# A four-block transformer on one core: TensorE's order in the tile loop around the gate of the first expert layer

## What is computed

```python
x = x + tanh(g_xattn[0]) * attention(layernorm(x), mask, ctx)       # 32 heads of 8, rotary, second softmax over ctx
x = x + tanh(g_ffn[0])   * top1_experts(layernorm(x))               # 8 experts, 256 -> 256, gate = softmax
x = x + tanh(g_xattn[1]) * wkv(layernorm(x), ctx)                   # recurrence over the 64 rows
x = x + tanh(g_ffn[1])   * top2_experts(layernorm(x))               # 8 experts, 256 -> 704 -> 256
```

## Time and profile before

| | |
|---|---|
| median of three runs | 498.18 us |
| profiled execution: its own time, its span | 498.84 us, 496.7 us |
| granted TensorE clock, mean | 0.994 |
| busy: TensorE (matmul), its weight loads, VectorE, ScalarE, GpSimd | 93%, 70%, 76%, 52%, 35% |
| tiles 1 to 6 on TensorE | about 52 to 249 us, 33.5 us each |

### The profile page before, as it was taken

How to read it: one execution, slowest core, us unless ns; L and a number is a source line. 1 busy time by engine, 2 the same in 40 slices (tenths; PEclk the granted TensorE clock), 3 DMA queues, 4 the chain that set the end, 5 groups by cost and what they waited for, 6 DMA issues and landing times. The chain is left out here.

```text
span 496.7 us, 10389 instructions
## 1 busy us (share of the span) xinstructions
PE 461.7 (93%) x3123; PEld 347.1 (70%) x3124; DVE 376.7 (76%) x1007; ACT 259.4 (52%) x562; POOL 175.8 (35%) x228
## 2 busy tenths in 40 slices
PE   4979999998999999999989999999999999999993
PEld 2648677686686776866857755566777878788782
DVE  5876788998988889989877889767867566566540
ACT  2765384572752845737513343326565766657641
POOL 4134213225124232241131160315446557555522
PEclk9999999999999999999999899999999999999998
DMA  7951304004022040040130689648566767768511
GB/s 217 287 107 29 63 1 86 18 13 86 22 44 53 21 84 15 12 84 16 38 69 21 255 341 366 193 116 298 170 205 215 251 183 245 223 197 252 162 22 21
DMA packets 24769, 63.37 MB, mean 128 GB/s; under 512 B 5176, under 2 KB 15296, under 8 KB 21792
## 3 DMA queue, kind: packets, MB, share of 16 engines
q1 hardware_dynamic: 19456, 56.38, 37.2%
q0 software_dynamic: 4416, 6.03, 6.6%
q10 hardware_dynamic: 864, 0.54, 0.3%
HBM read 48.79 MB, written 5.24 MB: 109 GB/s over the span
## 5 line engine op out<-in xcount | busy, mean ns | idle before, releaser
L2021 PE MATMUL bank_o<-w,hT 128*128 (+1 forms) x276 | 68.3, 389 | 1.9 <-issue 1.0
L1406 DVE TENSOR_TENSOR wl<-lw,wh 128x1024 fp32r<-128x1024 f32 (+1 forms) x54 | 60.9, 1129 | 1.1 <-ACT wh L639 1.1
L2021 PEld LDWEIGHTS bank_o<-w,hT 128*128 128x128 f32 (+1 forms) x276 | 48.8, 189 | 16.2 <-issue 11.4
L639 ACT ACTIVATE wh<-lw 128x1024 fp32r<-128x1024 f32 (+1 forms) x54 | 52.9, 981 | 1.8 <-DMA lw<-in_w 1.8
L1091 DVE TENSOR_REDUCE mx<-bank_s 128x8 f32<-128x512 f32 x64 | 42.6, 687 | 11.0 <-PE bank_s L1756 10.7
L498 POOL TENSOR_SCALAR rstd<-mv 128x1 f32<-128x1 f32 x32 | 9.3, 289 | 111.5 <-DVE mv L1011 111.5
L1754 PE MATMUL bank_s<-Kh,Qx 128*128 128x128 f32 x256 | 40.9, 282 | 1.5 <-DVE mx L1091 1.0
L593 POOL DMA_INDIRECT out_x<-ys,idx_out x18 | 29.0, 1609 | 35.3 <-ACT ys L911 33.6
L1754 PEld LDWEIGHTS bank_s<-Kh,Qx 128*128 128x128 f32 x256 | 35.8, 190 | 6.2 <-DVE mx L1091 3.3
L1399 DVE TENSOR_TENSOR hh<-sg,bank_s 128x256 f32<-128x256 f32 x46 | 19.0, 418 | 27.2 <-ACT sg L900 25.3
L1811 PEld LDWEIGHTS bank_o<-Vx,Pt 128*64 128x64 f32 x1024 | 32.5, 138 | 10.0 <-issue 5.5
(11 more groups left out here) (352 smaller groups left out, 1147.4 us busy)
## 6 DMA issues: line engine op xcount, KB each, us to landing
lw<-in_w SPq DMA_DIRECT2D x18, 1408.0 KB, 6.3
Q<-Qx SPq DMA_DIRECT2D x16, 512.0 KB
up<-in_w SPq DMA_DIRECT2D x5, 1408.0 KB, 7.4
w<-in_w SPq DMA_DIRECT2D x4, 1536.0 KB, 12.6
Pt<-in_WT SPq DMA_DIRECT2D x1, 1024.0 KB, 11.6
CT<-in_ctxT SPq DMA_DIRECT2D x1, 896.0 KB, 9.1
X<-in_x SPq DMA_DIRECT2D x1, 768.0 KB, 8.0
out_x<-X SPq DMA_DIRECT2D x6, 128.0 KB, 1.7
```

What stands on the lines that cost most here:

```text
L639: return act.activation(dst, src, ACT.Copy, scale=scale)
L1406: dve.tensor_tensor(wl[par][:, :, at:at + k], lw[par][:, :, at:at + k], wh[par][:, :, at:at + k].bitcast(F32), ALU.subtract).then_inc(w_lo, 1)
L2021: ins = pe.matmul(bo[:, 0:HID], hT[0:k, i, :], w2[0:k, bass.ts(e, 1), i, :].rearrange("p o n -> p (o n)"), start=(i == 0), stop=(i == IT - 1))
```

## The change

In TensorE's `tile`, and nowhere else: the projection of batch 1 stands right behind that of batch 0, ahead of `turn_h2`; one constant product stands between `turn_maxima` and `gate_logits`; the first scores of batch 0 are cut from their `attend` and stand between `turn_q` and `turn_comb`, with two constant products behind them; what is left of that `attend`, `low_and_shift`, stays where it was. The constant products write bank o. So tiles 1 to 6 have three matmuls more than before, and five instruction groups in another order.

```diff
                 project_kv(t + 1, 0)
+                project_kv(t + 1, 1)
                 turn_h2(t - 1)
                 turn_maxima(t)
+                constant_products(bo, 1)
                 gate_logits(t - 1)
                 turn_q(t + 1)
-                project_kv(t + 1, 1)
+                scores(t, par, 0, 0, True, True)
+                constant_products(bo, 2)
                 turn_comb(t - 1)
                 experts0(t - 1, 0)
                 experts0(t - 1, 1)
                 if prev2:
                     turn_y(t - 2)
-                attend(t, par, 0, True, True)
+                low_and_shift(t, par, 0, 0)
                 experts0(t - 1, 2)
                 experts0(t - 1, 3)
                 attend(t, par, 1, True, True)
```

## The result

The changed kernel takes 506.66 us (median of 4 runs, 505.69 to 509.87) against 498.19 for the kernel before beside it (4 runs, 497.85 to 498.54). The ratio is 1.018, with an interval of 1.013 to 1.023: slower, as forecast, but 1.5 us beyond the forecast and 0.06 above the top of its range. By how little it lies outside is chance: the changed kernel was timed 16 times in this study in three groups, and the medians of the other two groups (506.05 and 506.04) and of all 16 (506.2) lie inside the range, all about 1 us above the forecast. The profiled execution took 507.37 us with a span of 505.2.

The account below looks back on a forecast made before the run. TensorE and VectorE were taken as two chains in balance, meeting at comb. The norm turned late costs 7.5 us over six tiles, less 0.5 saved in tile 1: 498.18 + 7.0 = 505.2 us, range 502.4 to 506.6.

Parts of the forecast that it names:

- Comb 3.52 after the norm is turned: Gate chain, norm turned to comb's end: stays 3.52 us, so comb comes 1.25 us later in each tile.
- A wait of 0.3 before the first scores: TensorE, between q and comb: waits 0.3 us until batch 0's values are copied.
- One constant free before the logits: TensorE, before the gate's logits: 0.23 us constant product hidden in a 0.36 us wait, taken at nothing.
- The third pair of experts more than 1 us late and behind VectorE's mix: Third pair's start against batch 0's projection: at least 1 us later, after a wait of about 0.5 for the mix.
- The wait of 0.3 before comb: TensorE, after first scores and two constants: another wait of about 0.3 us before comb is turned.
- The sum for the loop was 7.0: Tiles 1 to 6: 7.5 us from the late norm, less 0.5 saved once in tile 1.
- TensorE had been free for it at just that time: Before the third pair, kernel before: TensorE free just as VectorE's first mix ended, so two chains in balance.
- The step that failed: Whole execution: the profiled execution's difference of 7.0 us was put on the 498.18 us median, giving 505.2.
- The first: Rival, third pair not held by the first mix: each tile saves 0.5, 502.7 us; 12%.
- The second: Rival, comb follows TensorE's stream, not the turned norm: -0.03 us a tile, 498.0 us; 4%.
- The third: Rival, VectorE's 3.5 us idle time a tile takes the delay up: 498.2 to 499 us; 3%.
- The fourth: Rival, TensorE's clock falls in each tile's changed stretch: would add 9 us, 514 us; 4%.

Follow-up runs that it names:

- e3: Changed kernel without its three constant products at the new place; 506.8 us, ratio 1.018 to the kernel before.
- e1: The changed kernel again, unedited (also written e1_again); 506.05 us, ratio 1.017 to the kernel before.
- e5: Changed kernel with constant matmuls of no use filling two start-up holes (eight and four); 506.92 us, ratio 1.016 to the kernel before.
- e11: The changed kernel unedited once more, on another chip; 506.04 us, ratio 1.017 to the kernel before.
- e13: Changed kernel with ScalarE's last two expert-weight conversions moved later in tile 0; 504.89 us, ratio 1.013 to the kernel before.
- e12: Kernel before with ScalarE's last two expert-weight conversions moved later in tile 0; 497.79 us, ratio 0.999.
- e7: Changed kernel with VectorE's reciprocal behind comb cut from 256 columns to 16; 503.29 us, ratio 1.008 to the kernel before.
- e8: Kernel before with VectorE's reciprocal behind comb cut from 256 columns to 16; 496.0 us, ratio 0.994.
- e6: Kernel before with constant matmuls of no use filling two start-up holes (eight and four); 500.7 us, ratio 1.005.
- e10: The kernel before unedited once more, on another chip; 498.7 us, ratio 1.002.
- e2: Kernel before with only batch 1's projection moved ahead of the turned norm, no moved scores or constants; 508.46 us, ratio 1.021.
- e9: Kernel before with only two of the four matmuls of batch 1's projection moved ahead of the turned norm; 500.07 us, ratio 1.005.
- e4: Changed kernel with batch 1's projection back below q, scores and constants still moved; 504.32 us, ratio 1.012 to the kernel before.

## Why the prediction was right, and where it was wrong

**The mechanism held, step by step.** No wait before the turned norm: there is none. A tile of 34.7 us: 34.7. Comb 3.52 after the norm is turned: 3.46. A wait of 0.3 before the first scores: 0.38, 1.9 us in six. One constant free before the logits: e3 shows all three of them free. VectorE's idle time before the logits' copy up by 1.2: 0.87 + 0.16, some 0.2 less. The third pair of experts more than 1 us late and behind VectorE's mix: 1.08 to 1.26 in tiles 2 to 6, with a wait of 0.33 where 0.5 stood. The wait of 0.3 before comb is half that: the constants' two slots end at 95.30 (94.84 + 2 x 0.23), and comb is turned at 95.46. The sum for the loop was 7.0, and the five profiles with the change's own loop (the first one, e1, e5, e11, e13) have 6.65 to 6.74. Its terms: the norm is turned 7.42 late in the sum, where 7.5 stood; tile 1 wins back 0.42, where 0.5 stood; and comb, which was to follow the norm by an unchanged 3.52, follows it by 3.46, which takes 0.3 off and was not in the sum. All three are small, and together they go the other way than the miss. One reading was incomplete without harm to the sum: "TensorE had been free for it at just that time" holds for the matmuls before the third pair, but the third pair's weight loads already waited for the mix there (0.27 us in tile 3, 0.29 in tile 2), so VectorE led at that handover before the change.

**The step that failed** is in the first paragraph: "the median of the three runs is 498.18, 0.66 lower. My sum is a difference inside the profiled execution, and I put it on the median", with a range made of the sum's own parts. It put all that is outside the six tiles at nothing, without a reason. In the profiled execution they held 1.8 of the span's 8.5 us (1.13 ahead of the loop, 0.63 behind it), and over all executions of both kernels about 1.4, if the loop takes in each what it takes in the profiles. Three runs of the kernel before agreed to 0.35 us and suggested so. Over all the runs of this study, 80 executions of the kernel before lie between 496.57 and 500.59 and 16 of the changed kernel between 503.29 and 509.87. A range that held this scatter would have reached some 2 us higher. That this group of four fell just outside the range, and the other two just inside, is luck; that all three lie about 1 us above the forecast is not explained by it.

**What remains open.** The means of those executions are 498.49 and 506.57, 8.1 us apart, with a standard error of 0.5; the loops are 6.7 apart. The pairs that share an edit give 7.1 (e12, e13), 7.3 (e7, e8, with loops 5.6 apart) and 6.2 (e5, e6). Less the loops' own difference that leaves 1.4 by the means, and 0.5, 1.7 and -0.4 by the pairs: about 1 us of the result that the profiled loop doesn't hold. Candidates are the start (55.50 and 53.33 in two profiles of the same kernel) and the first gather behind the loop, on which TensorE waited 0.6 us in the first profile of the kernel before and in e10, and 1.5 in the changed kernel's and in e11, but 0.5 in e1_again, and 2.5 in e6, which has the order of before. Neither goes with the change in every profile. That the change makes them worse on average was not shown, and was not ruled out. Nor is it known that the loop takes 202.1 us in the 13 of the changed kernel's 16 executions that have no profile. The clock alone doesn't explain the long ones: the mean granted clock was 0.993 at 509.87 us and 0.991 at 503.29.

**The rivals.** *The first*, that each tile saves 0.5 because VectorE doesn't hold the third pair, is refuted by the wait on the mix, 1.7 us in five tiles, and by e2 against the changed kernel: with the scores back in their old place tiles 2 to 5 are no longer and no shorter, so the move saves nothing there. In e7 against e8, with a shorter chain, the price falls from 6.7 to 5.6, which is still above that rival's 4.5; but VectorE holds the fourth pair there too. *The second*, that comb follows TensorE's stream, would have had comb within 2.97 of the norm; it is 3.46 in the changed kernel, 3.47 in e9. *The third*, that VectorE's idle time takes the delay up, gave 498.2 to 499: VectorE's busy time stayed at 30.0 in a tile of 34.7, so its idle time only grew. The rule of the Trainium skill ("Perfetto Trace Analysis", section "Identifying the Most-Contended Engine") would here have called TensorE's weight loads (73% of a tile) the less contended engine. The trace doesn't agree for this question: a change of TensorE's order alone cost 6.7 us. A share of busy time is a statement on one engine, and the two chains were bound to each other at comb. *The fourth*, the clock, had the wrong size and the wrong place: in the changed kernel it didn't fall in the loop at all, and in e2 and e3 it fell in one tile of six, for about 1.4 us, not by 9 us in all.

No kernel of these is better than the one before beyond doubt; e8 is faster only because it leaves work out.

## What to carry to other kernels

Before you fill an engine's wait with work from below, set the work's length against the wait (here 1.72 us against 0.3), and find what hangs on the instruction that you put it in front of: everything beyond the wait was paid by that chain here, once a tile. Then ask what the work covered where it stood. Here it was the cover of a chain of small steps of 3.5 us, and the work put in its place repaid next to nothing where VectorE's chain came behind it (tiles 2 to 6). Look at the weight loads' waits too, not only the matmuls'. And compare kernels by a length inside the trace that repeats (the loop, to 0.1 us in five profiles), not only by totals of which a few runs happened to agree.

## What was not expected of the hardware

- The clock fell in one tile of six that had the same order and the same waits. In e3 the wait before comb was only 0.53 us in tile 1, less than the 0.71 of e9, which kept 1.00, and the pair of experts behind it took 1.19 where the changed kernel's takes 0.70. Where it fell it cost about 1.4 us (the excess of e3's loop over e1_again's, 203.54 - 202.08 = 1.46).
- The same load from memory landed between 26.2 and 29.2 us in different executions. Its lateness was not passed on at par: e4's was 1.2 later than that of the kernel before, and its tile 1 began 4.2 later; from 35 to 45 us TensorE had run at 1.2 GHz. And the clock fell in the start-up of e10 (0.75 from 35 to 40 us) and e13 (0.50) though TensorE waited only 0.42 us for q.
- With matmuls put into such a hole the clock was 1.00 from 30 to 55 us in both profiles, but tile 1 began 1.6 us later in e6 than in the kernel before (55.97, 54.37), and the median rose by 1.8 us. In the changed kernel they did not pay either (506.92, and 506.05 on the same chip without them).
- TensorE's weight loads can wait where the matmuls behind them show no wait: 2.6 us in ten places of the kernel before, and with those waits gone in e8 its loop was 1.13 us shorter.
